# Identity matmuls in idle places, one PSUM bank in place of two in three cores, other orders in the slots of a four-block network kernel

## The reference

```
x = x + 0.5 * _L0_ffn_ref(_layernorm(x, axis=-1), ...)
x = x + _L0_attn_ref(_layernorm(x, axis=-1), ...)
x = x + 0.5 * _L0_ffn_ref(_layernorm(x, axis=-1), ...)
...
x = x + 0.5 * _L3_ffn_ref(_layernorm(x, axis=-1), ...)
x = x + _L3_attn_ref(_layernorm(x, axis=-1), ...)
x = x + 0.5 * _L3_ffn_ref(_layernorm(x, axis=-1), ...)
```

## Time and profile before

| | us |
|---|---|
| median of three runs | 3175.35 (3172.24 to 3183.04) |
| profiled execution, its own time | 3180.55 |
| span of its instructions | 3178.7 |
| TensorE busy | 2708.7 |
| VectorE busy | 2222.8 |
| ScalarE busy | 1704.1 |
| GpSimd busy | 799.8 |
| mean granted clock | 0.897 |

### The profile page before, as it was taken

The page is one execution under the profiler, slowest core; times in us unless marked ns, Lnnn a source line. Parts: engine busy times, 40 slices in busy tenths (PEclk is TensorE's granted clock), DMA queues, the critical chain, the costliest instruction groups (busy, mean ns, idle before and its releaser), DMA issues.

```text
span 3178.7 us, 64037 instructions
## 1 busy us (share of the span) xinstructions
PE 2708.7 (85%) x24501; PEld 1719.0 (54%) x24561; DVE 2222.8 (70%) x5316; ACT 1704.1 (54%) x4158; POOL 799.8 (25%) x809
## 2 busy tenths in 40 slices
PE   5867788899987789998877888899998888999996
PEld 2645455544444544467855787566663332556664
DVE  4656567778876667765566446888787777788883
ACT  2235443565622366643357434677775566776772
POOL 1010001111111211101222114655441112555540
PEclk8767787899986799998899989999998888999997
DMA  2523310000000000036700466010100000101010
GB/s 106 221 38 69 67 48 1 1 1 1 1 1 1 1 1 1 10 111 238 245 19 1 152 229 204 18 26 16 26 16 2 1 1 1 24 16 26 17 33 11
DMA packets 134794, 159.36 MB, mean 50 GB/s; under 512 B 82901, under 2 KB 109781, under 8 KB 132954
## 3 DMA queue, kind: packets, MB, share of 16 engines
q1 hardware_dynamic: 131962, 150.08, 15.5%
q0 software_dynamic: 2048, 4.20, 0.4%
q10 hardware_dynamic: 480, 0.98, 0.1%
HBM read 106.53 MB, written 30.61 MB: 43 GB/s over the span
## 4 chain that ended last, share of the span: by engine, by line
PE 49%; DVE 22%; ACT 10%; issue 6%; POOL 4%; DMA 3%; SPq 0%; DVEq 0%; POOLq 0%; ACTq 0%; another core or an unknown queue 0%
DVE nm L1190 5%; PE ps L1149 4%; PE ps L534 3%; PE ps L1922 3%; PE ps L2124 3%; PE ps L1126 3%; ACT hand L498 3%; PE ps L1090 3%; PE ps L2290 3%; PE ps L387 2%; PE ps L611 2%; PE ps L266 2%; DVE pre L2210 2%; PE ps L1520 2%; PE ps L2427 2%
## 5 line engine op out<-in xcount | busy, mean ns | idle before, releaser
L1190 DVE TENSOR_REDUCE nm<-ps 128x2 f32<-128x256 f32 (+2 forms) x704 | 424.8, 636 | 97.8 <-PE ps L1090 54.7
L1239 ACT ACTIVATE core<-ps 128x512 f32<-128x512 f32 x672 | 359.3, 589 | 91.4 <-PE ps L1131 55.8
L328 POOL TENSOR_TENSOR rstd<-ve,weights 128x4 f32<-128x4 f32 x80 | 81.1, 1014 | 941.5 <-DVE ve L305 921.7
L2196 POOL TENSOR_TENSOR pre<-pre,sin 128x512 f32<-128x512 f32 x128 | 238.1, 1881 | 258.3 <-ACT pre L2167 218.1
L1090 PE MATMUL ps<-hand 128*128 128x128 bf16 (+4 forms) x989 | 236.7, 316 | 42.0 <-DVE nm L1190 37.7
L498 ACT COPY hand<-ps 64x512 bf16<-64x512 bf16 x336 | 194.9, 580 | 135.4 <-PE ps L534 86.9
L1126 PE MATMUL ps<-hand 128*128 128x128 bf16 (+4 forms) x999 | 214.1, 304 | 11.6 <-ACT hand L498 6.3
L2330 ACT ACTIVATE core<-ps,nm 128x128 f32<-128x128 f32 x512 | 182.2, 377 | 68.3 <-DVE nm L2347 67.8
L2201 POOL TENSOR_TENSOR ss<-ss,weights 128x16 f32<-128x16 f32 x64 | 196.4, 3068 | 71.0 <-DVE ss L2216 69.1
L2124 PE MATMUL ps<-weights,pre 128*128 128x512 f32 x384 | 205.1, 637 | 5.8 <-ACT pre L2170 3.4
L1149 PE MATMUL ps<-core,hand 128*32 128x512 f32 (+3 forms) x2048 | 181.7, 450 | 8.1 <-ACT otok L1222 4.1
(11 more groups left out here) (346 smaller groups left out, 6695.8 us busy)
## 6 DMA issues: line engine op xcount, KB each, us to landing
hand<-in_experts SPq DMA_DIRECT2D x72, 836.0 KB, 4.9
shear<-post SPq DMA_DIRECT2D x64, 256.0 KB
core<-in_experts SPq DMA_DIRECT2D x16, 836.0 KB, 7.4
core<-shear SPq DMA_DIRECT2D x128, 64.0 KB, 2.3
hand<-hand SPq DMA_DIRECT2D x16, 512.0 KB, 4.4
hand<-hand SPq DMA_DIRECT2D x16, 384.0 KB, 5.6
pre<-sorted_in SPq DMA_DIRECT2D x8, 704.0 KB, 6.1
sorted_out<-core SPq DMA_DIRECT2D x88, 64.0 KB
```

The costliest lines, as they stand in the source:

```text
L1190: nc.vector.tensor_reduce(nm_of(unit), src, AX.X, ALU.max, negate=True).then_inc(negmax, 1)
L1239: nc.scalar.activation(prob8[:, i % PROBS, 0:w], m.ps[:, RING[at % NR], 0:w], ACT.Exp).then_inc(ring_out, 1)
L2196: ins = nc.gpsimd.tensor_tensor(o[:, :, :, z:z + hl], x[:, :, :, y0:y0 + hl], sn[:, t, :, z:z + hl].unsqueeze(2).to_broadcast([P, 2, LH, h ...
```

## The change

There are four edits.

1. **Fillers.** A stream of matmuls that multiply the identity by itself (bf16, 128 rows, 256 output columns) and whose result nobody reads. They write into the upper half of a bank that is free in that slot: `FILL_AT` says which bank during which core. An added letter in the tensor order of a slot sets how many stand where. There are 1180 of them: 81 in slot -1, 68 in slot 3, 85, 96, 119 and 126 in slots 4 to 7, 18 in slot 9, 119, 99, 63 and 79 in slots 16 to 19, 67 in slot 32, 61 in slot 34, and 99 in slot 56. Other slots have none. The first filler of a slot waits for the core before it.
2. **Single banks.** `l0_attn_core` turns into one bank, `l1_attn_core` gathers in one, `l2_ffn_core` writes its tiles to one. Each time TensorE now waits for the copy of the unit just before, where it waited for the one before that.
3. **Orders.** In 31 of the slots from 3 on, the order of at least one of TensorE, VectorE, ScalarE or GpSimd is another one (13 with fillers, and slots 10, 15, 20, 22, 24, 25, 33, 39 to 41, 43, 47 to 49 and 51 to 54 without). Slots -1 to 2 and 56 were woven before; they have orders now.
4. **A way to start the next slot's steps early** (upper-case letters), which no order here uses.

```
+def fillers(nc, m, bank, n):
+    out = m.ps[:, bank, L - FILL:L].rearrange("p (a b) -> p a b", b=P)
+
+    def tensor(pe):
+        for _ in range(n):
+            yield 0.0
+            nc.tensor.matmul(out, m.identb, m.identb.unsqueeze(1).to_broadcast([P, FILL // P, P]), start=True, stop=True)
+
+    return [(1.0, dict(tensor=tensor))]
...
+FILL = 256
+FILL_AT = {"l0_ffn": 4, "l0_attn": 3, "l1_attn": 5, "l2_ffn": 5}
...
@@ l0_attn_core
-    S, PT, O = (0, 1), (2, 3), (4, 5)
+    S, PT, O = (0, 1), 2, (4, 5)
...
-            if u >= 2:
-                pe.wait_ge(pT_ready, u - 1)
+            if u >= 1:
+                pe.wait_ge(pT_ready, u)
...
@@ l1_attn_core
-                out = m.ps[:, 4 + g % 2, t * P:(t + 1) * P]
+                out = m.ps[:, 4, t * P:(t + 1) * P]
+                if i == 1:
+                    pe.wait_ge(state_ready, NT - 1)
...
-                if t == 0 and g >= 2:
-                    pe.wait_ge(o_out, g - 1)
+                if t == 0 and g >= 1:
+                    pe.wait_ge(o_out, g)
...
@@ l2_ffn_core
-            if i >= 2:
-                pe.wait_ge(out_ready, i - 1)
+            if i >= 1:
+                pe.wait_ge(out_ready, i)
...
@@ one order of 58, slot 5, TensorE
-    {"tensor": "b1a1b1c1b1c1b1a1b1a1c1b1a2b3a2b1c1a2b1a1b1c1a2b2a2b1a1b1a2b1c1a7",
+    {"tensor": "b1c1a1b1e2c1e1b1e5b1e3b1e1a1e2a1e2c1e24b1e9b1e9b1e7a1e3b1e2a3b1a1c1e3b1e2a2b1e2a1e3b1e1c1e3a1e1b1"
+               "a2b1a1b1c1b1a3e1a2e5a3e5a1",
```

More of the change, by code:

```diff
@@ L188, in program, with started, in_order @@
         begun += span
-def in_order(name, eng, streams, order):
+def started(name, eng, streams):
     steps = [program(stream, name, eng) for stream in streams]
-    for s in steps:
-        next(s, None)
+    for step in steps:
+        next(step, None)
+    return steps
+def in_order(name, eng, streams, order, begun=None, following=None, gate=None):
+    steps, ahead = begun or started(name, eng, streams), None
     for i, n in runs(order):
+        if i < 0 and ahead is None:
+            gate(eng)
+            ahead = started(name, eng, following)
         for _ in range(n):
-            next(steps[i], None)
+            next(steps[i] if i >= 0 else ahead[i + AHEAD], None)
+    return ahead
+AHEAD = ord("a") - ord("A")
 def runs(order):
@@ L227, in weave, with merge @@
             first[0] = max(t, first[0])
-def merge(name, eng, streams, orders):
+def merge(name, eng, streams, orders, begun=None, following=None, gate=None):
     if name in orders:
-        in_order(name, eng, streams, orders[name])
-    else:
+        return in_order(name, eng, streams, orders[name], begun, following, gate)
+    if begun is None:
         weave(name, eng, streams)
+FILL = 256
[7 more added lines that the diff above has]
+    return [(1.0, dict(tensor=tensor))]
 def slot(nc, notes, streams, orders):
@@ L1733, in scalar @@
                 before.read(act)
-            nc.scalar.copy(a.otok[:, g, :], bank(m, 4 + g % 2)).then_inc(o_out, 1)
+            nc.scalar.copy(a.otok[:, g, :], bank(m, 4)).then_inc(o_out, 1)
     def done(eng):
@@ L2728 @@
      "scalar": "a5b1a1b1a1b1a1b2a2",
-     "gpsimd": "c1b1"},
-    {},
+     "gpsimd": "c1b1",
+     "sync": "b2"},
+    {"tensor": "a4b64a1b3a2b7a1b4a1b8a1b6a1b7a1",
+     "vector": "a12",
+     "scalar": "a5",
+     "gpsimd": "a1",
+     "sync": "a2"},
 ]
@@ L3120, in streams_of @@
                 streams.append((nothing, [(1.0, dict(gpsimd=keep))]))
-            return [(after, parts) for after, parts in streams if parts]
+            streams = [(after, parts) for after, parts in streams if parts]
+            bank = FILL_AT.get(names[units[k][0]]) if 0 <= k < len(units) else 2
+            if k == len(units) - 1:
+                bank = 6
+            if bank is not None and k != 1:
+                order = ORDERS[SLOT_ORDERS[k]].get("tensor", "") if k in SLOT_ORDERS else ""
+                n = sum(c for i, c in runs(order) if i == len(streams))
+                streams.append((before.pre if k == len(units) - 1 else before.core, fillers(nc, m, bank, n)))
+            return streams
         for k in range(-1, first):
@@ L3136, in all_slots, with gate @@
         def all_slots(name, eng):
+            ahead = None
             for k, streams in slots:
-                merge(name, eng, streams, ORDERS[SLOT_ORDERS[k]] if k in SLOT_ORDERS else {})
-                if first + 2 <= k < len(units):
-                    eng.wait_ge(cleared, k - first - 1)
+                def gate(eng, early=True):
+                    if first + 2 <= k < len(units):
+                        eng.wait_ge(cleared, k - first - 1)
+                        if early:
+                            eng.sem_inc(opened, 1)
+                ahead = merge(name, eng, streams, ORDERS[SLOT_ORDERS[k]] if k in SLOT_ORDERS else {}, ahead,
+                              slots[k - first + 1][1] if k < len(units) else None, gate)
+                if ahead is None:
+                    gate(eng, False)
                 eng.sem_inc(passed[name], 1)
```

355 lines of the change are left out of this document (198 added, 157 removed), and 7 rows, old and new, of the table SLOT_ORDERS.

## The result

| | before | after |
|---|---|---|
| median of three runs, us | 3175.35 | 3129.34 (3125.07 to 3137.15) |
| profiled execution, its own time, us | 3180.55 | 3125.07 |
| span of its instructions, us | 3178.7 | 3123.3 |
| mean granted clock | 0.897 | 0.946 |

The ratio of the times is 0.985, with a 95% interval of 0.983 to 0.988. That is 46 us faster, where 50 was forecast. Measured again, beside the last group of experiments, the changed kernel stood at 0.987 (0.984 to 0.989). As the experiments show, the forecast came that close because two misses cancelled.

The account below looks back on a forecast made before the run. About half the time waits for matmuls, whose time depends on the granted clock, low for a fifth of the run. Terms -9 - 51 + 5 + 1 + 4 = -50 us took 3175.35 to 3125 us, range 3070 to 3166.

Parts of the forecast that it names:

- Last slot, -9: Last slot: fillers keep TensorE from resting, clock stays at 1.00, line 2427 and last groups run faster; -9 us (0 to -10).
- Other filled slots, -51: Twelve other filled slots from slot 3 on: fillers collect 60% of what full clock could save; -51 us.
- the prize: Twelve other filled slots: the most that full clock could save, 284 x 0.6 / 2 = 85 us.
- What fillers cost, +5: Filler runs delay matmuls when results come early, but most waits outlast the run; +5 us (0 to 120).
- Slot -1, +1: Slot -1: 17 of 81 fillers may delay the first matmul by up to a microsecond, gain nil; +1 us.
- Single banks, +4: Three cores: TensorE waits for the previous unit's copy, mostly a wait moved ahead; together +4 us (0 to 54).
- Other orders, 0: 18 slots without fillers get other orders; 1 us a slot allowed in either direction, taken as 0.
- the fourth: Rival: fillers stand on the chain and make the kernel slower; +22 us, 3197 us, chance 0.08.
- the fifth: Rival: the other orders outweigh the rest of the change; 3125 +- 20 us or more, chance 0.07.
- The first: Rival: clock held nearly everywhere, all 85 us collected, costs of 6; -88 us, 3087 us, chance 0.25.
- the second: Rival: clock doesn't follow, fillers too few, except at the end; -12 us, 3163 us, chance 0.12.
- the third: Rival: single-bank waits replace the low clock, costing 27 us instead of 4; -27 us, 3148 us, chance 0.08.

Follow-up runs that it names:

- the new head: The kernel of before with new orders in slots -1 to 3 alone, without any filler; 3158.33 us, 0.9944 of before (0.992 to 0.997).

## Why the prediction came out right, and where it didn't

- **Last slot, -9.** Right: 46.2 to 36.3 us with the whole change, 37.4 by itself, and the clock at 1.00 with the product at 1.10 us.
- **Other filled slots, -51.** The share of the low time that comes back was right (60% forecast, 66% measured). The worth of a microsecond of low clock was near: 0.30 forecast, 0.33 over the executions of the kernel before, 0.37 in slot 18. So the prize was 94 to 105 us rather than 85, and 62 to 69 of it came back.
- **What fillers cost, +5.** This is the step that failed. The text said that "they stand at waits of which most are longer than the run". In slots 4 to 7 they are 11 to 15% of the chain. The cost in the eight attention slots alone is 30 to 42 us, and doubling the fillers added 44. The 0.12 us per filler was right. What was wrong was the belief that a filler in front of a wait is hidden. The waits were read from the trace of the old orders, and the change's own orders took most of the longest kind away: 15.3 us in three waits for line 450 became 4.2 in one in slots 4 to 7. Some 33 of the 94 us of fillers there and in slots 16 to 19 found no idle time, and runs of 27 and 35 fillers stand on the chain. The whole term, gain and cost together, was forecast at -46 and came to between -22 and -26 (31 to 35 by the ratios, less 9 for the last slot).
- **Slot -1, +1.** Small, and rather the other way. The 17 fillers ahead of the first matmul delayed nothing: it begins at 17.39 us, where it was 17.46. The slots up to 1 are about a microsecond shorter with the 81 fillers than without, which is no more than executions differ by.
- **Single banks, +4.** About 8 by the ratios, 4.7 of it in slots 4 to 7. The upper end for this core, 16, was reached under the old orders: 16.5 us measured. But it was reached in another way than told, by twelve waits of up to 3.2 us and not by 28 of 0.58. The cover named, `weigh` right behind the turn, is not what hides the wait; the new orders are.
- **Other orders, 0.** The second step that failed: 19 us, 12 of it from slots 1 and 2. The term went through the 18 slots from 3 on and was right for these. It left out slots -1 to 2, though their change from a woven to a written order was in the description. The trace of before had VectorE's wait of 5.4 us for line 983 in slot 2 to be read. The clock gain that came with the new head, about half of the 6.3 us in slot 2, was in no term either.
- **The total.** -9 - 26 + 8 - 19 = -46. These are steps from one kernel to the next, so they sum to the whole by themselves. The fillers gave 20 us less than forecast and the orders 19 more, and that the total was near is luck. Of the rivals, the fourth (fillers on the chain) holds in part, with 30 to 42 us of the 55 from which on it would have decided, and the fifth (orders that weigh in) as well. The first is out, since a third of the low time stayed and the fillers cost more than its 6 us. The clock followed, so the second is out, and the banks took no more than 8 us, so the third is out.

Of the signs named ahead, the last slice, line 2427, the clock above 0.88 and 0.12 us a filler came true. The 5 us for each of the eight slots did not: 0.5 us each in slots 4 to 7 and 3.4 each in slots 16 to 19. A sign of the fifth rival came true: slots 1 and 2, which have no fillers, moved by 6 us each.

What stays open: the profiled spans differ by 55.4 us, of which 13.8 lie ahead of slot 3, 15.0 in the filled slots, 9.9 in the last stretch, and 16.7 in slots that have no fillers. Two executions of the changed kernel differ by 12.1 us, most of it in such slots too, so how much of the 16.7 is the change's was not settled.

## What to carry to other kernels

A filler is free only while the wait it stands in outlasts it, and that wait has to be read with the new orders in place, not in the trace from before them. Read its share of the chain in the profile after, not its share of idle time before, and double the count once in a trial: here the same number again took everything back. Where a change rewrites the order of work, cost every stretch whose order changes, those that a generator used to weave above all. Look there for the longest waits of the busiest engines. And profile the same kernel twice before reading anything from a difference of some microseconds in one slot.

## What the hardware showed that was not expected

- Slot 18, the same instructions in the same order, took 44.4 us in one execution and 50.6 in another, with the granted clock at 0.96 and 0.80. Where the low stretches fall differs between executions of one kernel.
- The low clock costs 0.37 us per microsecond in slot 18 and about 0.33 over the whole kernel before, though TensorE was busy for 38.15 of slot 18's 44.4 us at the high clock.
- Another order of the same instructions ran at a higher granted clock without any filler: 0.87 in slot 2, where the woven order ran at 0.72 in one execution and at 0.83 in another.
- A 128-column filler, half the work of a 256-column one, has a mean duration of 240 ns against 283. The 1180 of them took 57 us less of busy time and held the clock of slots 4 to 7 at 0.88 instead of 0.93.
